# ScalarE in place of VectorE for row scalings with a column as bias, and for two roundings, in a cross-attention and small-attention kernel

## The reference

```python
# first layer: cross-attention, 16 heads of 64
lat = layer_norm(_layernorm(x), ln_lat_g, ln_lat_b);  ctx = layer_norm(context, ln_ctx_g, ln_ctx_b)
q = lat @ Wq;  k, v = split(ctx @ Wkv);  k = apply_rope(k, cos, sin)
attn = softmax(clip(q k^T * 64 ** -0.5, -11, 11), axis=-1)
x = x + (attn @ v) @ Wo + bo
# second layer, on l = _layernorm(x)
h = _rmsnorm(l, gamma1)
q = h @ Wq2 + bq;  k, v = split((h @ Wdown + bdown) @ Wup + bup)     # 16 heads of 8
l = l + softmax(q k^T / sqrt(8)) v @ Wo2 + bo2                       # heads of one token attend to each other
h2 = _rmsnorm(l, gamma2);  gate = softmax(h2 @ Wg + bg)
l = l + sum over 8 experts of gate_e * (h2 @ We[e])
x = x + l
```

## Time and profile before

| | before |
|---|---|
| median of 3 runs | 323.86 us (323.68 to 324.25) |
| profiled execution, its own time | 325.46 us |
| its span, first to last instruction | 323.6 us |
| TensorE busy | 296.0 us, 91% |
| VectorE busy | 244.1 us, 75%, 449 instructions |
| ScalarE busy | 163.3 us, 50%, 325 instructions |
| GpSimd busy | 207.7 us, 64%, 207 instructions |
| mean granted TensorE clock | 0.977 of full |

### The profile page before, as it was taken

The page is one execution under the profiler, slowest core; times in us unless marked ns, Lnnn a source line. Parts: engine busy times, 40 slices in busy tenths (PEclk is TensorE's granted clock), DMA queues, the critical chain, the costliest instruction groups (busy, mean ns, idle before and its releaser), DMA issues.

```text
span 323.6 us, 6610 instructions
## 1 busy us (share of the span) xinstructions
PE 296.0 (91%) x2478; PEld 205.7 (64%) x2478; DVE 244.1 (75%) x449; ACT 163.3 (50%) x325; POOL 207.7 (64%) x207
## 2 busy tenths in 40 slices
PE   5858999999999999998999999999999999989693
PEld 4736666666668766665777666556786665666551
DVE  2957998675874849899878798976737698588916
ACT  2525645668442735564416465764446467034441
POOL 5415785565572839686636577598737587856964
PEclk9795999999999999999999999999999999999979
DMA  7844112211210111111111111111101200000001
GB/s 206 245 118 110 43 51 65 68 32 36 57 26 18 35 32 34 32 35 34 39 26 34 35 32 34 32 35 32 34 7 28 51 1 2 0 2 1 0 18 32
DMA packets 16319, 14.24 MB, mean 44 GB/s; under 512 B 4832, under 2 KB 11808, under 8 KB 16288
## 3 DMA queue, kind: packets, MB, share of 16 engines
q1 hardware_dynamic: 15088, 13.62, 16.2%
q10 hardware_dynamic: 1200, 0.20, 0.3%
HBM read 4.89 MB, written 0.52 MB: 17 GB/s over the span
## 4 chain that ended last, share of the span: by engine, by line
PE 52%; DVE 21%; issue 8%; POOL 7%; ACT 5%; DMA 4%; SPq 2%; POOLq 0%; ACTq 0%; DVEq 0%
PE pv L624 12%; PE sc L610 10%; PE sums L645 6%; PE side L735 4%; PE pj_k L548 3%; DMA kswap<-ksin 2%; PE pj_k L550 2%; PE pj_k L549 2%; DMA sin_in<-in_L_xattn_sin_dram 2%; SPq L516 2%; ACT e L905 2%; DVE ksin L1286 2%; POOL e L1705 2%; DVE ks L1222 2%; PE side L810 2%
## 5 line engine op out<-in xcount | busy, mean ns | idle before, releaser
L1705 POOL TENSOR_SCALAR e<-e 128x1024 f32<-128x1024 f32 x64 | 71.0, 1110 | 66.2 <-ACT e L905 59.4
L905 ACT ACTIVATE e<-sc 128x1024 f32<-128x1024 f32 x64 | 65.6, 1025 | 33.2 <-PE sc L610 33.2
L610 PEld LDWEIGHTS sc<-qs,ks 64*128 64x128 f32 x768 | 50.8, 189 | 27.3 <-issue 22.9
L610 PE MATMUL sc<-qs,ks 64*128 64x256 f32 x768 | 63.8, 299 | 3.1 <-ACT e L905 2.2
L624 PE MATMUL pv<-e,v 128*64 128x256 f32 x512 | 62.3, 385 | 0.6 <-ACT u L913 0.6
L1698 POOL TENSOR_TENSOR krot<-kcos,kswap 128x512 f32<-128x512 f32 x32 | 44.0, 1376 | 11.3 <-DMA kswap<-ksin 8.7
L624 PEld LDWEIGHTS pv<-e,v 128*64 128x64 f32 x512 | 34.1, 136 | 22.9 <-issue 6.8
L913 ACT ACTIVATE u<-pv 128x256 f32<-128x256 f32 x32 | 12.3, 385 | 61.0 <-PE pv L624 61.0
L1222 DVE TENSOR_TENSOR ks<-krot,ks 128x512 fp32r<-128x512 f32 x32 | 31.1, 971 | 0.0
L1286 DVE TENSOR_TENSOR ksin<-pj_k,sinT 128x512 f32<-128x512 f32 x32 | 21.9, 684 | 5.8 <-POOL krot L1698 3.6
L897 ACT ACTIVATE v<-pj_k 128x512 f32<-128x512 f32 x28 | 16.5, 600 | 13.9 <-PE pj_k L550 13.5
(11 more groups left out here) (307 smaller groups left out, 579.4 us busy)
## 6 DMA issues: line engine op xcount, KB each, us to landing
kswap<-ksin SPq DMA_DIRECT2D x128, 64.0 KB, 2.0
ctx_in<-in_ctx_dram SPq DMA_DIRECT2D x4, 256.0 KB, 2.9
prod<-in_L_xattn_Wkv_dram SPq DMA_DIRECT2D x2, 512.0 KB, 6.8
x_in<-in_x_dram SPq DMA_DIRECT2D x1, 512.0 KB, 6.7
prod<-in_L_xattn_Wq_dram SPq DMA_DIRECT2D x1, 512.0 KB, 7.5
wo<-in_L_xattn_Wo_dram SPq DMA_DIRECT2D x1, 512.0 KB, 6.9
fwe<-in_L_ffn_We_dram SPq DMA_DIRECT2D x1, 512.0 KB, 4.1
out_dram<-x_in SPq DMA_DIRECT2D x3, 128.0 KB, 1.8
```

The lines of the kernel that those rows point to most:

```text
L610: last = nc.tensor.matmul(sc[:, h, c * NT:(c + 1) * NT], ks[rows, j % 3, k_part, chunk], qs[rows, j % 2, q_part, :], start=(k_part + q_par ...
L905: nc.scalar.activation(e[:, j % 3, :, 2 * half:2 * half + 2, :].rearrange("p h c n -> p h (c n)"), sc[:, :, :], ACT.Exp, scale=SCALE).then ...
L1705: nc.gpsimd.tensor_scalar(a, a, EXP_HIGH, EXP_LOW, ALU.min, ALU.max).then_inc(s_clip, 1)
```

## The change

ScalarE computes `Identity(scale * row + bias)` with two columns, rstd and off = -mean * rstd, where VectorE computed (row - mean) * rstd: contexts and tokens of batches 1 to 3 (`prepare`, p = 2, at the end of the slot), hn at (3, a) and xl at (3, end) for batches 0 to 2 of the second layer, and hn2 with a scale alone at (11, end). It also rounds the transposed contexts and tokens to their high parts for batches 1 to 3, before `attention_copy` in slots p = 4 and p = 6. VectorE keeps the low parts, now after `key_lo`. GpSimd makes the offsets, two more instructions for each. Batch 0's preparation and the tail stay as they were. The diff, without declarations of buffers and semaphores and without the removed VectorE functions, which the functions above show:

```diff
-    "layer_norm": [(3, "first")],
+    "layer_norm": [(3, "a")],
+    "layer_norm_last": [(3, "end")],
...
+                    rows = x_in[:, TT * b:TT * b + TT, :]
+                    if stands("layer_norm", b, slot, place):
+                        act.wait_ge(s_rr1, b + 1)
+                        scaled(hn, rows, rr1, hn_off, TT).then_inc(s_hn, 1)
+                    if stands("layer_norm_last", b, slot, place):
+                        if b >= 2:
+                            act.wait_ge(s_x23, b - 1)
+                        act.wait_ge(s_frstd, b + 1)
+                        scaled(xl[:, b % 2, :, :], rows, f_rstd, xl_off, TT).then_inc(s_xl, 1)
+                    if stands("root_norm", b, slot, place):
+                        act.wait_ge(s_rr2, b + 1)
+                        for t in range(TT):
+                            last = nc.scalar.activation(hn2[:, t, :], xl[:, b % 2, t, :], ACT.Copy, scale=rr2[:, t:t + 1])
+                        last.then_inc(s_hn2, 1)
+
+            def scaled(dst, src, rstd, off, n):
+                for t in range(n):
+                    last = nc.scalar.activation(dst[:, t, :], src[:, t, :], ACT.Identity, scale=rstd[:, t:t + 1],
+                                                bias=off[:, t:t + 1])
+                return last
+
+            def prepare(b, p):
+
+                if p == 2:
+                    act.wait_ge(s_crstd, b + 1)
+                    act.wait_ge(*made("ctx_T", b - 1))
+                    scaled(ctx_n, ctx_in[:, b % 2, :, :], c_rstd, c_off, SC).then_inc(s_ctxn, 1)
+                    act.wait_ge(s_lrstd, b + 1)
+                    act.wait_ge(*made("lat_T", b - 1))
+                    scaled(lat_2, x_in[:, TT * b:TT * b + TT, :], l_rstd, l_off, TT).then_inc(s_latn, 1)
+                if p == 4:
+                    act.wait_ge(*taken("ctx_T", b))
+                    if b >= 2:
+                        act.wait_ge(s_kproj, PAIRS * (b - 1))
+                        act.wait_ge(s_vproj, 8 * (b - 1))
+                    nc.scalar.activation(ctxT[:, b % 2, 0, :], ctxT_f[:, :], ACT.Copy).then_inc(s_ctxThi, 1)
+                if p == 6:
+                    act.wait_ge(*taken("lat_T", b))
+                    act.wait_ge(s_qproj, PAIRS * b)
+                    nc.scalar.activation(latT[:, 0, :], latT_f[:, :], ACT.Copy).then_inc(s_latThi, 1)
...
                 if 0 <= slot + 1 < NPAIR:
                     query_hi(slot + 1)
+                b, p = divmod(slot, PAIRS)
+                if 0 <= b < NB - 1 and p >= 4:
+                    prepare(b + 1, p)
+                second_layer(slot, "a")
                 if 1 <= slot <= NPAIR:
                     attention_copy(slot - 1)
...
                 if 0 <= slot + KV_AHEAD < NPAIR:
                     key_hi(slot + KV_AHEAD)
+                if 0 <= b < NB - 1 and p == 2:
+                    prepare(b + 1, p)
                 second_layer(slot, "end")
...
+            def split_ctxT(b):
+                hi, lo = ctxT[:, b % 2, 0, :], ctxT[:, b % 2, 1, :]
                 if b:
-                    dve.wait_ge(*made("lat_T", b - 1))
-                normalise(lat_2, x_in[:, TT * b:TT * b + TT, :], l_mv, l_rstd, TT).then_inc(s_latn, 1)
-
-            def split_ctxT(b):
-                dve.wait_ge(*taken("ctx_T", b))
-                if b >= 2:
-                    dve.wait_ge(s_kproj, PAIRS * (b - 1))
-                    dve.wait_ge(s_vproj, 8 * (b - 1))
-                hi, lo = ctxT[:, b % 2, 0, :], ctxT[:, b % 2, 1, :]
-                own(nc.vector.tensor_copy(hi, ctxT_f[:, :]))
+                    dve.wait_ge(s_ctxThi, b)
+                else:
+                    dve.wait_ge(*taken("ctx_T", b))
+                    own(nc.vector.tensor_copy(hi, ctxT_f[:, :]))
                 split_lo(lo, ctxT_f[:, :], hi).then_inc(s_ctxT, 1)
             def split_latT(b):
-                dve.wait_ge(*taken("lat_T", b))
                 if b:
-                    dve.wait_ge(s_qproj, PAIRS * b)
-                own(nc.vector.tensor_copy(latT[:, 0, :], latT_f[:, :]))
+                    dve.wait_ge(s_latThi, b)
+                else:
+                    dve.wait_ge(*taken("lat_T", b))
+                    own(nc.vector.tensor_copy(latT[:, 0, :], latT_f[:, :]))
                 split_lo(latT[:, 1, :], latT_f[:, :], latT[:, 0, :]).then_inc(s_latT, 1)
...
-                if more and p == 4:
-                    split_ctxT(b + 1)
...
                 if 0 <= slot + 1 < NPAIR:
                     query_lo(slot + 1)
+                if 0 <= slot + 1 < NPAIR:
+                    key_lo(slot + 1)
+                if more and p == 4:
+                    split_ctxT(b + 1)
                 if more and p == 6:
                     split_latT(b + 1)
-                if 0 <= slot + 1 < NPAIR:
-                    key_lo(slot + 1)
...
+            def offset(dst, mean, rstd):
+                own(nc.gpsimd.tensor_scalar(dst, mean, -1.0, None, ALU.mult))
+                return nc.gpsimd.tensor_tensor(dst, dst, rstd, ALU.mult)
+
             def ctx_rstd(b):
                 pool.wait_ge(s_cstat, b + 1)
-                inverse_root(c_rstd[:, :], c_mv[:, :, 1], LN_EPS).then_inc(s_crstd, 1)
+                last = inverse_root(c_rstd[:, :], c_mv[:, :, 1], LN_EPS)
+                if b:
+                    own(last)
+                    last = offset(c_off[:, :], c_mv[:, :, 0], c_rstd[:, :])
+                last.then_inc(s_crstd, 1)
...
-                        two_norms(rr1[:, :], f_mv[:, :, 1], RMS_EPS).then_inc(s_rr1, 1)
-                        inverse_root(f_rstd[:, :], f_mv[:, :, 1], LN_EPS).then_inc(s_frstd, 1)
+                        own(two_norms(rr1[:, :], f_mv[:, :, 1], RMS_EPS))
+                        offset(hn_off[:, :], f_mv[:, :, 0], rr1[:, :]).then_inc(s_rr1, 1)
+                        own(inverse_root(f_rstd[:, :], f_mv[:, :, 1], LN_EPS))
+                        offset(xl_off[:, :], f_mv[:, :, 0], f_rstd[:, :]).then_inc(s_frstd, 1)
```

More of the change, by code:

```diff
@@ L336, in xattn_ffn @@
         half_p = sb("half_p", [128, SC])
+        c_off = sb("c_off", [128, SC])
+        l_off = sb("l_off", [128, TT])
+        hn_off = sb("hn_off", [128, TT])
+        xl_off = sb("xl_off", [128, TT])
         sc = es.enter_context(nc.psum_tensor("sc", [128, 2, 512], fp32))
@@ L379, in xattn_ffn @@
         s_ctxT = sem("s_ctxT")
+        s_ctxThi = sem("s_ctxThi")
+        s_latThi = sem("s_latThi")
         s_latT = sem("s_latT")
@@ L1245, in ctx_normalise @@
                 dve.wait_ge(s_crstd, b + 1)
-                if b:
-                    dve.wait_ge(*made("ctx_T", b - 1))
                 normalise(ctx_n, ctx_in[:, b % 2, :, :], c_mv, c_rstd, SC).then_inc(s_ctxn, 1)
@@ L1524, in layer_norm_statistics @@
                 statistics(f_mv, f_stat, [tokens(b)[:, t, :] for t in range(TT)]).then_inc(s_fstat, 1)
-            def layer_norm(b):
-                dve.wait_ge(s_rr1, b + 1)
-                normalise(hn, tokens(b), f_mv, rr1, TT).then_inc(s_hn, 1)
-                if b >= 2:
-                    dve.wait_ge(s_x23, b - 1)
-                dve.wait_ge(s_frstd, b + 1)
-                normalise(xl[:, b % 2, :, :], tokens(b), f_mv, f_rstd, TT).then_inc(s_xl, 1)
-            def root_norm(b):
-                dve.wait_ge(s_rr2, b + 1)
-                for t in range(TT):
-                    last = nc.vector.tensor_scalar(hn2[:, t, :], xl[:, b % 2, t, :], rr2[:, t:t + 1], None, ALU.mult)
-                last.then_inc(s_hn2, 1)
             def second_layer(slot, when):
@@ L1548, in second_layer @@
                         layer_norm_statistics(b)
-                    if stands("layer_norm", b, slot, when):
-                        layer_norm(b)
                     if stands("products_0", b, slot, when):
@@ L1578, in second_layer @@
                         reduce_outputs(1).then_inc(s_o2, 1)
-                    if stands("root_norm", b, slot, when):
-                        root_norm(b)
                     if stands("gates", b, slot, when):
@@ L1630, in _ @@
                         tokens_statistics(b + 1)
-                    if p == 2:
-                        ctx_normalise(b + 1)
-                        tokens_normalise(b + 1)
                 if p == 2 and 1 <= b <= NB:
@@ L1669, in tokens_rstd @@
                 pool.wait_ge(s_lstat, b + 1)
-                two_norms(l_rstd[:, :], l_mv[:, :, 1], LN_EPS).then_inc(s_lrstd, 1)
+                last = two_norms(l_rstd[:, :], l_mv[:, :, 1], LN_EPS)
+                if b:
+                    own(last)
+                    last = offset(l_off[:, :], l_mv[:, :, 0], l_rstd[:, :])
+                last.then_inc(s_lrstd, 1)
             def mean_square_root(dst, ss):
```

1 line of the change is left out of this document (removed).

## The result

| | before | after |
|---|---|---|
| median of 4 runs each | 324.06 us (323.68 to 324.55) | 335.72 us (334.62 to 339.07) |
| ratio | | 1.0376, 95% interval 1.0339 to 1.0413 |
| profiled execution, span | 323.6 us | 332.7 us |
| VectorE busy | 244.1 us, x449 | 220.1 us, x409 |
| ScalarE busy | 163.3 us, x325 | 177.8 us, x365 |

What follows compares the result with a forecast made beforehand. TensorE's in-order queue was taken to bound the kernel between warm-up and tail. Terms 0.54 + 0.53 + 0.80 + 2.05 + 2.2 + 2.2 - 0.9 = 7.4 us on 323.86 gave 331.3 us, range 327.0 to 334.5.

Steps and rivals of the forecast that it cites:

- The price of a tile: One 128x128 ScalarE pass with scale and bias columns, in a row: 0.38 us, bounds 0.305 and 0.49.
- oT: End of slot 18: six tiles delay ScalarE's copy oT, which out_proj2 reads; +2.05 us (1.6 to 2.7).
- slot 11: Six tiles at the end of slot 10 delay the exponential and the scores' second half: +0.53 us.
- slot 12: The xl pair ahead of hT, with hn's share, delays query_down: +0.80 us (0.6 to 1.0).
- slot 20: root_norm at the end of slot 19 waits for rr ahead of hT, delaying query_down: +2.2 us (1.7 to 2.5).
- ctx_T: With xl off VectorE, the side bank ahead of ctx_T is freed earlier: gain 0.2 us (0 to 0.2).
- the waits were not absorbed: Against the rival that waits on rr and oT are absorbed and passes alone count: +3.7 us, 327.6 us, chance 0.14.
- no relief of VectorE showed: Against the rival that a relieved VectorE brings differences and GpSimd's passes sooner: 320.6 us, chance 0.05.
- rival (4): Worse than forecast: tiles do not overlap, 0.49 us each; 10.6 us slower, 334.5 us, chance 0.10.
- Slot 28: root_norm at the end of slot 27 waits for rr ahead of hT, delaying query_down: +2.2 us (1.7 to 2.5).
- Slot 3: Six tiles at the end of slot 2 delay the next exponential and what follows: +0.54 us.
- The gain at recS: The cast of latT leaves VectorE's chain ending in recS: gain 0.7 of TensorE's 1.0 us wait (0 to 1.0).

Runs made afterwards that it cites:

- the runs on it: The first kernel with later statistics, with batch 1's six tiles a slot later: 322.82 us; or with those tiles back on VectorE and their offsets gone: 322.91 us.
- the kernel with idle products: The changed kernel with 11 extra identity products on TensorE just before query_down in slots 20 and 28: 331.59 us, ratio 1.0256.
- the kernel with root_norm later: The changed kernel with root_norm moved from the end of slot 11 to slot 12 place a, behind hT: 331.03 us, ratio 1.0194.
- that with the six tiles alone: The kernel before with only batches 1 to 3's context and token tiles on ScalarE at slots' ends, with GpSimd offsets: 329.63 us, ratio 1.0151.
- the kernel with the offsets alone: The kernel before with GpSimd's offsets added for every batch, read by nobody: 330.78 us, ratio 1.0162.
- the first kernel with later statistics: The changed kernel with all ScalarE steps off the slots' ends and VectorE's statistics of batches 2 and 3 behind the norm bank's taking: 322.73 us, ratio 0.9951.
- that with batch 1's tiles a slot later: The first kernel with later statistics, with batch 1's six tiles in slot 3 instead of slot 2: 322.82 us, ratio 0.9972.
- kernel with root_norm alone: The kernel before with only root_norm (hn2) on ScalarE, at the end of slots 19 and 27 ahead of hT: 329.11 us, ratio 1.0129.

## Why the prediction was wrong

**What held.** The sign, and the frame: TensorE's queue is the length of the kernel, VectorE's 24 us are worth almost nothing, and what counts is what ScalarE's queue holds back. The price of a tile (0.38 against 0.385 us), oT (+2.05 against +2.01), slot 11, slot 12, slot 20 (+2.2 against +2.22) and ctx_T came as worked out. The rivals fell: the waits were not absorbed, no relief of VectorE showed, and tiles did overlap, so that rival (4), the nearest in time, had the wrong reason.

**The step that failed** is the sum: it takes a wait of TensorE to cost its own length. Behind the waits of 2.13 and 2.77 us the granted clock fell to the 1.2 GHz level, and the work that followed cost 1.54 and 2.63 us more. With TensorE kept busy through the same delays 4.1 us of the 11.7 were gone. On the medians the forecast is short by 4.3 us. In the account of the two profiled executions it is short by 3.6: the two falls give 4.2 us, the terms of the queue come to 8.5 us instead of 7.4 (the smaller steps below), and the tail's full clock, which is luck of one execution, takes 1.7 back. So the medians' 4.3 us are not the falls alone, though their size is nearly that. The falls could have been foreseen from the trace before, where TensorE at 24.40 us has been idle for longer and the clock is at half behind it, and once more at 307.71 us. TensorE, and busy time by stretch, in the kernel before:

```profile
24.40 0.50 PE L548 MATMUL pj_k<-ctxT,wkA 128*128 128x512 f32 x1 [2.79 <-DVE kcos L1286]
...
28.93 1.65 PE L610 MATMUL sc<-qs,ks 64*128 64x256 f32 x12 [0.18 <-ACT e L905]
```

```profile
24.00:28.00 4.00, 2.82 (x16) 2.10 (x17) 3.90 (x6) 1.71 (x4) 1.55 (x2) 0.65 0.52 142
28.00:32.00 4.00, 3.81 (x18) 2.64 (x18) 2.10 (x3) 2.55 (x4) 2.35 (x3) 0.50 0.33 86
```

These scores take 1.65 us against 0.98 elsewhere. I read the granted clock only around the edited places, where before it is 1.00, and not where TensorE had already stood still. The Trainium skill, "TensorE: Matmul & The Clock Gate", section "What's actually happening", has the mechanism, a gate on the clock that recent activity of the engine opens; the rows agree, in that each stretch at half clock here begins in or behind an idle time of TensorE. They also show that not every such idle time is followed by one.

**Smaller steps.** Slot 28 was mis-sized, +2.72 against +2.2: GpSimd's offsets push its rotation and both clips. GpSimd after:

```profile
249.32 0.71 POOL L1687 TENSOR_TENSOR xl_off<-xl_off,f_rstd 128x2 f32<-128x2 f32 x1
250.00 1.28 POOL L1738 TENSOR_TENSOR krot<-kcos,kswap 128x512 f32<-128x512 f32 x1
251.36 2.17 POOL L1745 TENSOR_SCALAR e<-e 128x1024 f32<-128x1024 f32 x2
```

No pause is left between the two clips, where before the second began after 1.47 us of idling. The work on rr starts only behind them, at 253.60 us. The prediction named this as a possible 0.7 us and left it out of the sum; it belonged in. Slot 3, +0.79 against +0.54, was near in size by luck and wrong in cause, as the runs on it show. The gain at recS did not come: the wait is 0.91 us against 1.0. The cast of latT, 0.69 us, left the chain, but two fp32 instructions in it (the key difference and the difference att) took 1.06 and 1.04 us instead of 0.68 and 0.76, which takes back all but 0.03; that GpSimd beside them is the reason was not tried.

One reading was wrong without touching the sum. The prediction sets VectorE's 0.50 us for ctx_n against ScalarE's 0.38 and calls each tile a gain of engine time. The 0.50 is a mean: in the profile before, 13 of the 16 ctx_n passes take 0.33 to 0.34 us, and the three that stand beside GpSimd's rotation or clip 1.06 to 1.29. VectorE in the profile before, where GpSimd does nothing beside it:

```profile
165.33 1.11 DVE L1235 TENSOR_SCALAR ctx_n<-ctx_in,c_mv,c_rstd 128x128 f32<-128x128 f32 x4
```

Four passes take 1.11 us there, so one follows the other after 0.26 us. ScalarE's 0.385 us beats only the disturbed passes.

**The expected signs.** Six tiles in a row, the waits for oT and hT and for rr, and both busy times came as written; the recS wait and the length of the last hT wait did not.

## What to carry to other kernels

Price a wait of the engine that bounds the kernel twice: its length, and the work behind it at the lower clock, for which the trace before had two examples, where that engine had already stood still. A second look is due before two profiles are subtracted: a stretch at half clock in one of them only, as in the tail here, is no effect of the change. Moving work to an idle engine is decided by what stands behind it in that engine's queue: the same instructions cost 11.7 us at the ends of slots and nothing that can be measured where the engine waited anyway. A helper instruction on a third engine is priced by everybody who waits for its result or for that engine next, and its price changes when the consumer moves.

## What the runs showed of the hardware

Behind TensorE's waits in the loop the granted clock stayed at 1.00 for 0.88, 1.44, 1.46 and 1.65 us, and went to the 1.2 GHz level for 1.93, 2.13 and 2.77 us. At 2.05 us both occur: the oT wait kept the clock in the profile after and in the kernel with idle products, and lost it in the kernel with root_norm later and in that with the six tiles alone; a wait of 2.05 us in slot 27 of the kernel with the offsets alone kept it. Longer waits do both as well: the tail's wait of 2.71 us lost the clock before and kept it after, and the same wait, 2.72 and 2.73 us long, kept it in the first kernel with later statistics and in that with batch 1's tiles a slot later. At the program's start, where TensorE pauses often, a wait of 1.54 us (kernel with root_norm alone, at 8.01 us) was followed by half clock from 9.61 us on. The wait of 2.7 to 3.3 us near 24 us lost the clock in all thirteen profiles. So the length of a wait alone doesn't tell whether an execution pays.

The loss behind one wait was 1.4 to 2.6 us in the loop, and 1.7 us in the tail. A kernel spreads by it: 334.62 to 339.07 us in the four runs after, and 322.92 to 325.92 us in 17 runs of the kernel before, which has such waits at 24.40 and 307.71 us.

A ScalarE pass of 128x128 with a scale and a bias column lasts 0.48 us, and in a row of six the next starts after 0.385 us. VectorE's pass for the same work lasted 0.33 to 0.34 us in the profile before, with the next 0.26 us later, also beside a GpSimd power on 128x2, and 1.06 to 1.30 us beside GpSimd's 128x512 rotation or its 128x1024 clip.
